# Normalisation of the later chunks moved into the steps of an expert layer, ranks from one comparison of all pairs

## The chip, the cores and the metric

The kernel runs on one core of a Trainium2 chip. The metric is the device time of one execution in microseconds (us), as the median of several runs. A core has five engines that work side by side and wait for each other through semaphores: TensorE (PE in the profile, with its weight loads as PEld), VectorE (DVE), ScalarE (ACT), GpSimd (POOL) and SyncE (SP, which here only issues DMAs). Each engine executes its own instructions in the order in which the program wrote them.

## The reference

x has 16 sequences of 128 tokens of width 128. Eight layers follow each other, each of the form x = x + tanh(gate) * f(layernorm(x)). The change concerns layer 0, a mixture of eight experts whose routing comes from the context, and the normalisation in front of layer 1, a feed-forward layer with quantised values.

```python
def _layernorm(x, axis=-1, eps=1e-05):
    m = jnp.mean(x, axis=axis, keepdims=True)
    v = jnp.var(x, axis=axis, keepdims=True)
    return (x - m) / jnp.sqrt(v + eps)
...
x = x + jnp.tanh(g_xattn[0]) * _L0_xattn_ref(_layernorm(x, axis=-1), ctx_1024, L0_xattn_Wg, L0_xattn_bg, L0_xattn_W1, L0_xattn_b1, L0_xattn_W2, L0_xattn_b2)
x = x + jnp.tanh(g_ffn[0]) * _L0_ffn_ref(_layernorm(x, axis=-1), L0_ffn_w1, L0_ffn_b1, L0_ffn_w2, L0_ffn_b2)
```

As the kernel computes layer 0: the logits of the eight experts are context times Wg plus a bias, for each token; the two experts with the highest logits are kept (the rank of an expert is the number of experts above it, a tie going to the lower number), the softmax over these two gives the weights `comb`; each expert is relu(n W1 + b1) W2 + b2, and the weighted sum over the experts, times tanh of the gate, is added to x.

## The kernel before

x is held transposed in `xT` (128 features on the partitions, 2048 tokens in the free dimension) and worked on in four chunks of 512 tokens. The normalised x is `nT`.

**Normalisation** (`pe_norm`, `act_norm`, `dve_norm`). For one chunk: PE multiplies by a centring matrix (L204), ACT squares the result into `nT` (L222), PE averages over the features (L209), ACT takes Ln and Exp to get one over the root (L226, L227), DVE multiplies (L235). Each float32 matmul of 512 columns is two instructions in the trace. In layer 0 DVE then splits the result into two float16 parts in `x16` (L241, L243; semaphores `s_hi`, `s_lo`). The four chunks are interleaved in the order of `ORDER`. In layers 0 and 1 all four chunks are normalised before the layer's own loop begins: `pe_norm` ends with a wait for all four.

**Layer 0** (`pe_moe`, `act_moe`, `dve_moe`) has 32 steps k, chunk c = k // 8 and expert e = k % 8. In step k PE makes 12 matmuls of 512 columns for the hidden values (`up`, L308), waits before each group of three that ACT has read that bank, and then the 48 matmuls of the second product of step k - 1 (`down`, L336). In the first step of a chunk PE waits for `s_lo`, the split part of that chunk. ACT reads each of the four banks twice, into float32 (L364) and float16 (L365). DVE subtracts the two to get the low part (`lo`, L378, `dve_moe_lo`), and adds the product of a step into `acc` with the expert's weight (L394 or L396). In DVE's loop the order of step k is: low part of the weights of expert k + 2 in chunk 0 (L284), low parts of step k + 1, wait for `down` of step k, accumulate step k. After the second step of the next chunk PE transposes `acc` and adds b2 (`pe_moe_out`, L349 and L350, eight pairs of 128 columns), and DVE updates `xT` (L405), which is `s_x`. In the fifth step of a chunk `comb` is transposed (L324), ACT copies it out one step later (L373).

The weights come in float32 through the four places of `stage`, and are split into float16 parts: the high part of expert 0 by DVE (L279) and of the others by ACT (L295), the low part by DVE (L284).

After step 0's `up` PE multiplies the context for the logits (L314). DVE adds the bias (L429), prepares the exponent (L432), and counts ranks with three small instructions for each expert (L437, L439, L441), 24 in all with a memset; then `lo` of step 1, the threshold, `comb` (L443 to L450), accumulation of step 0 and the low weights of expert 3.

**Layer 1** after its norm: per chunk 4 matmuls (L469), keys and values of layer 2 (L549, L551), the second product of the chunk before (L479). POOL gathers rows of a table in between, two in each step of layer 0, eight after it, and then spreads keys for layer 2 (L706).

SP issues all loads in the order of the program; the loads of experts 4 to 7 wait for a free place of `stage`.

## Time and profile before

| | |
|---|---|
| median of 3 runs | 948.12 us (942.97 to 950.73) |
| the profiled execution, device time | 939.63 us |
| its span from first to last instruction | 937.8 us |
| granted TensorE clock, mean | 0.931 of full |
| PE busy | 808.9 us, 86% of the span |
| DVE, ACT, POOL busy | 626.8, 570.3, 289.8 us |

Layer 0 with its norm fills the first 227 us of the span, layer 1 the time to about 265 us; the rest of the kernel, 673 us, is not edited. Busy times overlap: what sets the end is the chain of waits, followed from the last instruction back. A matmul's time depends on the granted clock, which has two levels, 1.2 and 2.4 GHz; 1.00 in a row is the upper one. Numbers of a profile are those of one execution.

### The profile page before, as it was taken

The numbers are of one execution on the slowest core, as the hardware profiler recorded it, in microseconds if no ns is written. First come the engines' busy times: TensorE is split into PE (matmuls) and PEld (weight loads), VectorE is DVE, ScalarE is ACT, GpSimd is POOL, SyncE is SP. The second block draws the span as 40 slices with busy tenths as digits, with TensorE's granted clock in tenths as the row PEclk, the third lists the DMA queues.
The fourth block names the chain that finished last, engine by engine and source line by source line (L and its number), as shares of the span: only waits on it lengthen the run. The fifth ranks groups of instructions, "written<-read, shape, count | busy, mean of one in ns | idle before, by whom it ended". The sixth has DMA issues, their size and how long they took to land.

```text
span 937.8 us, 14730 instructions
## 1 busy us (share of the span) xinstructions
PE 808.9 (86%) x5849; PEld 510.5 (54%) x5857; DVE 626.8 (67%) x994; ACT 570.3 (61%) x985; POOL 289.8 (31%) x253
## 2 busy tenths in 40 slices
PE   4899999999887888999939989968989868888775
PEld 1576767675433554555529656545668834444322
DVE  3896666663467778398784687854976246777567
ACT  5797878784664676545552433525588456666564
POOL 1043343432427777440030321034970012000003
PEclk9899999998997999999968997967999989999889
DMA  6121000002500001110000000060000000000001
GB/s 233 52 85 27 24 24 24 24 24 72 54 0 24 22 22 32 30 31 7 0 1 1 1 0 2 0 227 0 1 2 1 1 0 1 0 1 1 0 0 45
DMA packets 12852, 25.69 MB, mean 27 GB/s; under 512 B 3560, under 2 KB 4848, under 8 KB 12528
## 3 DMA queue, kind: packets, MB, share of 16 engines
q1 hardware_dynamic: 8688, 16.36, 6.0%
q0 software_dynamic: 4096, 8.40, 3.6%
q8 instruction: 46, 0.75, 0.4%
q14 instruction: 22, 0.18, 0.1%
HBM read 23.69 MB, written 1.05 MB: 26 GB/s over the span
## 4 chain that ended last, share of the span: by engine, by line
PE 58%; DVE 20%; ACT 12%; POOL 4%; issue 4%; DMA 1%; SPq 0%; DVEq 0%; POOLq 0%; ACTq 0%
PE ps L336 9%; PE ps L308 8%; PE ps L859 6%; PE ps L1025 3%; POOL big L706 2%; POOL pe L966 2%; PE ps L1377 2%; PE ps L204 2%; PE ps L578 2%; PE ps L1347 2%; DVE big L1112 2%; PE ps L469 2%; ACT nT L226 1%; ACT nT L227 1%; PE ps L1061 1%
## 5 line engine op out<-in xcount | busy, mean ns | idle before, releaser
L966 POOL DMA_INDIRECT pe<-in_rpe,idx x128 | 136.3, 1065 | 201.6 <-PE ps L336 114.1
L378 DVE TENSOR_TENSOR big<-l1f_w,big 128x512 f16<-128x512 f32 x128 | 87.4, 692 | 45.0 <-ACT big L365 42.8
L364 ACT ACTIVATE l1f_w<-ps,wcols 128x512 f32<-128x512 f32 x128 | 90.0, 703 | 32.8 <-PE ps L308 30.2
L308 PE MATMUL ps<-vx,big 128*128 128x512 f16 x384 | 94.7, 400 | 2.7 <-DVE nT L235 2.7
L336 PE MATMUL ps<-big 128*128 128x128 f16 x1536 | 92.6, 221 | 4.8 <-DVE big L378 4.8
L336 PEld LDWEIGHTS ps<-big 128*128 128x128 f16 x1536 | 89.9, 99 | 12.6 <-DVE big L378 5.5
L365 ACT ACTIVATE big<-ps,wcols 128x512 f16<-128x512 f32 x128 | 90.5, 707 | 0.0
L308 PEld LDWEIGHTS ps<-vx,big 128*128 128x128 f16 x384 | 38.1, 102 | 46.4 <-issue 8.7
L859 PE MATMUL ps<-nT,l1f_w 128*128 128x512 f32 x128 | 57.6, 592 | 0.0
L765 ACT ACTIVATE big<-ps 128x1024 f32<-128x1024 f32 x32 | 32.7, 1023 | 35.0 <-PE ps L575 35.0
L1642 POOL TENSOR_TENSOR big<-l1f_w,big 128x512 f16<-128x512 f32 x8 | 10.1, 1269 | 138.7 <-ACT big L1679 138.7
L1094 ACT ACTIVATE big<-ps,small 128x128 f32<-128x128 f32 x128 | 35.0, 379 | 26.3 <-PE ps L1052 26.2
L781 DVE TENSOR_REDUCE small<-ps 128x16 f32<-128x1024 f32 x32 | 38.8, 1218 | 8.8 <-PE ps L569 8.8
L204 PE MATMUL ps<-xT,consts 128*128 128x512 f32 x56 | 34.8, 729 | 11.3 <-DMA xT<-in_xT 10.3
L235 DVE TENSOR_TENSOR nT<-ps,nT 128x512 f32<-128x512 f32 x28 | 19.3, 690 | 37.2 <-ACT nT L227 37.2
L983 POOL TENSOR_TENSOR big<-nT,consts 128x512 f32<-128x512 f32 x16 | 17.4, 1098 | 84.8 <-PE ps L1042 44.5
L1025 PE MATMUL ps<-big,pe 128*128 128x128 f32 x256 | 32.3, 291 | 12.1 <-DVE big L1112 11.8
L578 PE MATMUL ps<-big 32*128 32x512 f16 x192 | 28.2, 399 | 15.8 <-POOL big L706 9.0
L886 ACT ACTIVATE big<-ps,wcols 128x1024 f32<-128x1024 f32 x16 | 17.9, 1116 | 39.0 <-PE ps L859 39.0
L1025 PEld LDWEIGHTS ps<-big,pe 128*128 128x128 f32 x256 | 31.8, 207 | 12.4 <-DVE big L1112 11.9
L1061 PEld LDWEIGHTS ps<-vx,big 128*128 128x128 f32 x256 | 34.2, 210 | 6.5 <-DVE big L1165 4.4
L209 PE MATMUL ps<-nT,consts 128*128 128x512 f32 x56 | 33.2, 677 | 3.7 <-ACT nT L222 3.6
(328 smaller groups left out, 1852.2 us busy)
## 6 DMA issues: line engine op xcount, KB each, us to landing
big<-in_l0x_w SPq DMA_DIRECT2D x16, 256.0 KB, 3.9
pe<-in_l2f_w SPq DMA_DIRECT2D x16, 256.0 KB, 6.4
pe<-in_rpe,idx POOLq DMA_INDIRECT x128, 2.6
cT<-in_cT SPq DMA_DIRECT2D x1, 1024.0 KB, 9.4
l1f_w<-in_l1f_w SPq DMA_DIRECT2D x1, 1024.0 KB, 5.1
vx<-in_ctok SPq DMA_DIRECT2D x1, 1024.0 KB, 16.7
out_xT<-xT SPq DMA_DIRECT2D x4, 256.0 KB, 2.3
xT<-in_xT SPq DMA_DIRECT2D x1, 768.0 KB, 7.5
```

The costliest lines, as they stand in the source:

```text
L204: te.matmul(bank(CEN[i] + c), centre_w, xT[:, cs(c)], start=True, stop=True).then_inc(s_cen, 1)
L308: mm = te.matmul(bank(f), w16[:, e, a, f * 128:(f + 1) * 128], x16[:, c, b, :], start=(n == 0), stop=(n == 2))
L336: mm = te.matmul(bank(4 + k % 2)[:, t * D:(t + 1) * D], h16[:, k % 2, a, f, t * S:(t + 1) * S], w16[:, k % E, b, F + f * D:F + (f + 1) * D ...
L364: act.activation(h32[:, f, :], bank(f), ACT.Relu, bias=b, scale=1 / W_UP)
L365: act.activation(h16[:, k % 2, 0, f, :], bank(f), ACT.Relu, bias=b, scale=1 / W_UP).then_inc(M0["act"], 1)
L378: dve.tensor_tensor(h16[:, k % 2, 1, f, :], h32[:, f, :], h16[:, k % 2, 0, f, :], SUB).then_inc(M0["lo"], 1)
L578: return te.matmul(bank(4 + t % 2), kT[quad(t), p, tok(b)], qblk1[quad(t), b % QS, r, :, :], start=(part == 0), stop=False)
L781: dve.tensor_reduce(mxp[:, b % 2, 2 * u:2 * u + 2, 0:8], ps[:, 1024 * u:1024 * (u + 1)].rearrange("p (t g k) -> p t g k", t=2, k=BLK), AX, ...
L859: mm = te.matmul(bank(at + r), l1f_w[:, w * D:(w + 1) * D], nT[:, cs(2 * (k // NC) + r)], start=True, stop=True)
L966: pool.indirect_dma_start(out=pe[:, v * D:(v + 1) * D], out_offset=None, in_=ins["rpe"], in_offset=bass.IndirectOffsetOnAxis(ap=idx[:, v:v ...
L1025: mm = te.matmul(bank(1 + f % 3)[:, j * 128:(j + 1) * 128], peT[:, f * VG + j, :], qblk[:, :, f * VG + j, :], start=True, stop=True)
L1061: mm = te.matmul(bank(6 + b % 2)[:, h * HW2:(h + 1) * HW2], cw[:, b % 2, h, :], vx4[:, b, h, :], start=True, stop=True)
```

## The change

In layer 0 only chunk 0 is normalised in front. Chunk c + 1 is centred in step e = 5 of chunk c (at its end on PE and on ACT) and averaged, turned into its factor and multiplied in step e = 6 (on DVE at the end of the loop's step, after the accumulation). The norm of layer 1 for chunk c - 1 stands in steps e = 2 and 3 of chunk c; that for the last chunk inside the first two rounds of layer 1's loop. Both use banks 6 and 7. `NORM_NO` numbers the eight norms in their new order.

The b2 product of `pe_moe_out` becomes one matmul of 512 columns instead of four of 128.

The ranks come from one comparison of all pairs (`above`, 1,024 elements a partition), seven small ones that replace "greater" by "greater or equal" where e is compared with a lower number, and one sum over 1,024 elements, which stands after the `lo` of step 1.

Loads: the constants needed in front come in a part of their own (192 KB of 440), with chunk 0 of x; expert 0's weights come next and have a semaphore of their own with the gates; then the context, experts 1 and 2, the gather's indices and the remaining constants, expert 3, and the rest of x. DVE makes the high part of expert 1's weights too. ACT's seven small copies of constants (L1775 to L1779) move from the start to behind layer 0.

```diff
@@ -184,12 +184,62 @@
         VAR = (2, 4, 6, 2, 0, 6, 0, 4)
         SPLIT = (0, 7)
 
+        NORM_NO = {(0, 0): 0, (0, 1): 1, (1, 0): 2, (0, 2): 3, (1, 1): 4, (0, 3): 5, (1, 2): 6, (1, 3): 7}
+
+        def late(k):
+            c, e = divmod(k, E)
+            if e in (5, 6) and c + 1 < NCH:
+                return ("cen", "var")[e - 5], 0, c + 1
+            if e in (2, 3) and c:
+                return ("cen", "var")[e - 2], 1, c - 1
+            return None, None, None
+
+        def pe_late_norm(te, k):
+            part, i, c = late(k)
+            if part == "cen":
+                n = NORM_NO[(i, c)]
+                if i:
+                    te.wait_ge(s_x, c + 1)
+                else:
+                    loaded(te, "x1")
+                    te.wait_ge(s_norm, n)
+                te.matmul(bank(6), centre_w, xT[:, cs(c)], start=True, stop=True).then_inc(s_cen, 1)
+            elif part == "var":
+                n = NORM_NO[(i, c)]
+                te.wait_ge(s_sq, n + 1)
+                if i == 0:
+                    te.wait_ge(M0["combT"], c)
+                te.matmul(bank(7), mean_w, nT[:, cs(c)], start=True, stop=True).then_inc(s_var, 1)
+
+        def act_late_norm(act, link, k):
+            part, i, c = late(k)
+            if part == "cen":
+                act.wait_ge(s_cen, NORM_NO[(i, c)] + 1)
+                act.activation(nT[:, cs(c)], bank(6), ACT.Square).then_inc(s_sq, 1)
+            elif part == "var":
+                act.wait_ge(s_var, NORM_NO[(i, c)] + 1)
+                link(act.activation(nT[:, cs(c)], bank(7), ACT.Ln, bias=eps5[:]))
+                act.activation(nT[:, cs(c)], nT[:, cs(c)], ACT.Exp, scale=-0.5).then_inc(s_rstd, 1)
+
+        def dve_late_norm(dve, k):
+            part, i, c = late(k)
+            if part == "var":
+                dve_scale(dve, i, c, bank(6))
+
+        def dve_scale(dve, i, c, centred):
+            n = NORM_NO[(i, c)]
+            dve.wait_ge(s_rstd, n + 1)
+            dve.tensor_tensor(nT[:, cs(c)], centred, nT[:, cs(c)], MUL).then_inc(s_norm, 1)
+            if i == 0:
+                dve.wait_ge(s_norm, n + 1)
+                dve.tensor_copy(x16[:, c, 0, :], nT[:, cs(c)]).then_inc(s_hi, 1)
+                dve.wait_ge(s_hi, c + 1)
+                dve.tensor_tensor(x16[:, c, 1, :], nT[:, cs(c)], x16[:, c, 0, :], SUB).then_inc(s_lo, 1)
+
         def x_done(layer, c):
             return NCH * layer + c + 1 if layer < 2 else 2 * NCH + BC * (c + 1) if layer == 2 else NCH * layer + B - NCH + c + 1
 
         def pe_norm(te, i, more=None):
-            if i == 0:
-                loaded(te, "const")
             if i == 4:
                 te.wait_ge(F3["best"], NC * NCH // 2)
                 te.wait_ge(F3["cand"], NC * NCH // 2)
...
@@ -274,10 +320,11 @@
             return ap.unsqueeze(2).to_broadcast([128, B, E])
 
 
-        def dve_first_parts(dve, link):
-            loaded(dve, "experts0", 4)
-            dve.tensor_scalar(w16[:, 0, 0, :], stage[:, 0, :], W_UP, None, MUL).then_inc(M0["w_hi"], 1)
-            dve_w_lo(dve, 0)
+        def dve_first_parts(dve, e):
+            if e:
+                loaded(dve, "experts0", 2)
+            dve.tensor_scalar(w16[:, e, 0, :], stage[:, e, :], W_UP, None, MUL).then_inc(M0["w_hi"], 1)
+            dve_w_lo(dve, e)
 
         def dve_w_lo(dve, e):
             dve.wait_ge(M0["w_hi"], e + 1)
...
@@ -317,9 +364,14 @@
                     pe_down(te, k - 1)
                 if e == 1 and c:
                     pe_moe_out(te, c - 1)
+                pe_late_norm(te, k)
                 if e == E // 2:
                     te.wait_ge(M0["comb"], 1)
                     te.wait_ge(X4["gkv"], 1)
+                    if c:
+                        te.wait_ge(s_rstd, NORM_NO[(1, c - 1)] + 1)
+                    else:
+                        loaded(te, "const")
                     for t in range(BC):
                         mm = te.transpose(ps[0:E, 3584 + t * S:3584 + (t + 1) * S], comb[:, c * BC + t, :], ident)
                     mm.then_inc(M0["combT_ps"], 1)
...
@@ -343,16 +395,21 @@
             te.wait_ge(M0["combT"], c + 1)
             if c:
                 te.wait_ge(s_x, c)
+                te.wait_ge(s_norm, NORM_NO[(1, c - 1)] + 1)
             loaded(te, "cols")
+            te.matmul(bank(6), l0x_b2[:], combT[:, cs(c)], start=True, stop=False)
             for t in range(BC):
-                dst = bank(6)[:, t * S:(t + 1) * S]
-                te.matmul(dst, l0x_b2[:], combT[:, tok(c * BC + t)], start=True, stop=False)
-                mm = te.matmul(dst, acc[:, t, :], ident, start=False, stop=True)
+                mm = te.matmul(bank(6)[:, t * S:(t + 1) * S], acc[:, t, :], ident, start=False, stop=(t == BC - 1))
             mm.then_inc(M0["out_ps"], 1)
 
-        def act_moe(act):
-            act.wait_ge(M0["w_hi"], 1)
-            act_w_hi(act, 1)
+        def act_moe(act, link):
+            act.wait_ge(s_set, 4)
+            act.wait_ge(s_cen, 1)
+            act.activation(nT[:, cs(0)], bank(4), ACT.Square).then_inc(s_sq, 1)
+            act.wait_ge(s_var, 1)
+            link(act.activation(nT[:, cs(0)], bank(2), ACT.Ln, bias=eps5[:]))
+            act.activation(nT[:, cs(0)], nT[:, cs(0)], ACT.Exp, scale=-0.5).then_inc(s_rstd, 1)
+            act.wait_ge(M0["w_hi"], 2)
             for k in range(NCH * E):
                 for f in range(FT):
                     act.wait_ge(M0["up"], FT * k + f + 1)
...
@@ -371,6 +428,7 @@
                 if k % E == E // 2 + 1:
                     act.wait_ge(M0["combT_ps"], k // E + 1)
                     act.activation(combT[:, cs(k // E)], ps[0:E, 3584:4096], ACT.Copy).then_inc(M0["combT"], 1)
+                act_late_norm(act, link, k)
 
         def dve_moe_lo(dve, k):
             for f in range(FT):
...
@@ -398,6 +456,7 @@
                 dve.wait_ge(M0["acc"], k + 1)
                 if e == 0 and c:
                     dve_moe_out(dve, c - 1)
+                dve_late_norm(dve, k)
             dve_moe_out(dve, NCH - 1)
 
         def dve_moe_out(dve, c):
...
@@ -406,21 +465,30 @@
 
 
         def pe_layer0(te):
-            pe_norm(te, 0)
+            loaded(te, "x0")
+            te.matmul(bank(4), centre_w, xT[:, cs(0)], start=True, stop=True).then_inc(s_cen, 1)
+            te.wait_ge(s_sq, 1)
+            te.matmul(bank(2), mean_w, nT[:, cs(0)], start=True, stop=True).then_inc(s_var, 1)
+            te.wait_ge(s_norm, 1)
             pe_moe(te)
 
         def act_layer0(act, link):
-            act_norm(act, link, 0)
-            act_moe(act)
+            act_moe(act, link)
+            loaded(act, "const")
+            act.activation(identb[:], ident, ACT.Copy).then_inc(s_g, 1)
+            act.activation(maskb[:], maskneg, ACT.Copy).then_inc(s_g, 1)
+            for j in range(4):
+                act.activation(keysb[:, j * S:(j + 1) * S], to_keys, ACT.Copy, scale=minus4[:, j:j + 1])
+            act.activation(hm16b[:], hm16, ACT.Copy).then_inc(s_g, 1)
 
         def dve_layer0(dve, link):
             loaded(dve, "cols")
-            loaded(dve, "gate")
+            loaded(dve, "gate_expert0")
 
             dve.tensor_tensor(ctx_w[:, E:], gate_w[:, 2 * NH2:4 * NH2], gate_w[:, 4 * NH2:6 * NH2], ADD).then_inc(X4["ctx_w"], 1)
-            dve_first_parts(dve, link)
-            dve_norm(dve, 0)
-            dve_w_lo(dve, 1)
+            dve_first_parts(dve, 0)
+            dve_scale(dve, 0, 0, bank(4))
+            dve_first_parts(dve, 1)
             dve_moe_lo(dve, 0)
             dve_w_lo(dve, 2)
             dve.wait_ge(M0["logit"], 1)
...
@@ -431,15 +499,13 @@
             link(dve.tensor_reduce(red, lg, AX, MAX))
             dve.tensor_tensor(ex, lg, per_b(red), SUB).then_inc(M0["exp_in"], 1)
 
-            link(dve.memset(sm(256), 0.0))
-            for e in range(E):
-                one = lg[:, :, e:e + 1]
-                link(dve.tensor_tensor(cmp, one.to_broadcast([128, B, E]), lg, ALU.is_gt))
-                if e < E - 1:
-                    link(dve.tensor_tensor(cmp[:, :, e + 1:], one.to_broadcast([128, B, E - 1 - e]),
-                                           lg[:, :, e + 1:], ALU.is_ge))
-                link(dve.tensor_tensor(rank, rank, cmp, ADD))
+            pairs = [128, B, E, E]
+            link(dve.tensor_tensor(above, lg.unsqueeze(2).to_broadcast(pairs), lg.unsqueeze(3).to_broadcast(pairs), ALU.is_gt))
+            for e in range(1, E):
+                ins_ = dve.tensor_tensor(above[:, :, e, 0:e], lg[:, :, 0:e], lg[:, :, e:e + 1].to_broadcast([128, B, e]), ALU.is_ge)
+            link(ins_)
             dve_moe_lo(dve, 1)
+            link(dve.tensor_reduce(rank, above, AX, ADD))
             link(dve.tensor_scalar(sm(256), sm(256), 2.0, None, ALU.is_lt))
             dve.wait_ge(M0["exp"], 1)
             link(dve.tensor_tensor(ex, ex, rank, MUL))
...
@@ -459,15 +525,21 @@
         o16 = work[:, 2048:2048 + CW].bitcast(f16).rearrange("p (r n) -> p r n", r=2)
 
         def pe_layer1(te):
-            pe_norm(te, 1)
             loaded(te, "l0f")
             for c in range(NCH + 1):
                 if c < NCH:
+                    te.wait_ge(s_norm, NORM_NO[(1, c)] + 1)
                     for f in range(FT):
                         if c:
                             te.wait_ge(F1["act"], FT * (c - 1) + f + 1)
                         te.matmul(bank(f), l0f_w1[:, f * 128:(f + 1) * 128], nT[:, cs(c)],
                                   start=True, stop=True).then_inc(F1["up"], 1)
+                    if c == 1:
+                        te.wait_ge(s_sq, 2 * NCH)
+                        te.matmul(bank(4), mean_w, nT[:, cs(NCH - 1)], start=True, stop=True).then_inc(s_var, 1)
+                    if c == 0:
+                        te.wait_ge(s_x, NCH)
+                        te.matmul(bank(5), centre_w, xT[:, cs(NCH - 1)], start=True, stop=True).then_inc(s_cen, 1)
                     pe_keys(te, c)
                 if c:
                     k = c - 1
...
@@ -475,13 +547,15 @@
                     te.wait_ge(F1["act"], FT * (k + 1))
                     if k >= 2:
                         te.wait_ge(F1["o16"], k - 1)
+                    else:
+                        te.wait_ge(s_norm, 2 * NCH)
                     for f in range(FT):
                         mm = te.matmul(bank(4 + k % 2), w2q[:, f, :], hq[:, k % 2, f, :],
                                        start=(f == 0), stop=(f == FT - 1))
                     mm.then_inc(F1["down"], 1)
 
         def act_layer1(act, link):
-            act_norm(act, link, 1)
+            last = nT[:, cs(NCH - 1)]
             loaded(act, "l0f")
 
             act.activation(w2q, l0f_w2.rearrange("p (t d) -> p t d", t=FT), ACT.Copy,
...
@@ -496,6 +570,13 @@
                             act.wait_ge(F1["down"], c - 1)
                         act.activation(hq[:, c % 2, f, :], bank(f), ACT.Relu, bias=col("l0f_b1", f),
                                        saturate=False).then_inc(F1["act"], 1)
+                    if c == 1:
+                        act.wait_ge(s_var, 2 * NCH)
+                        link(act.activation(last, bank(4), ACT.Ln, bias=eps5[:]))
+                        act.activation(last, last, ACT.Exp, scale=-0.5).then_inc(s_rstd, 1)
+                    if c == 0:
+                        act.wait_ge(s_cen, 2 * NCH)
+                        act.activation(last, bank(5), ACT.Square).then_inc(s_sq, 1)
                     act.wait_ge(A2["proj_ps"], 2 * c + 1)
                     act.activation(kT[:, 0, cs(c)], bank(6), ACT.Copy).then_inc(A2["hi"], 1)
                 if c:
...
@@ -506,8 +587,9 @@
                     act.activation(o16[:, k % 2, :], bank(4 + k % 2), ACT.Identity, bias=bq[:]).then_inc(F1["o16"], 1)
 
         def dve_layer1(dve, link):
-            dve_norm(dve, 1)
             for c in range(NCH + 1):
+                if c == 1:
+                    dve_scale(dve, 1, NCH - 1, bank(5))
                 if c < NCH:
                     dve_keys(dve, c)
                 if c:
...
@@ -1702,23 +1784,26 @@
         def _(sp):
             def load(k, dst, name, at=0):
                 sp.dma_start(dst, ins[name][:, at:at + dst.shape[-1]]).then_inc(s_load[k], 16)
-            sp.dma_start(idx[:], ins["idxT"]).then_inc(s_idx, 16)
-            load("const", consts[:], "consts")
+            load("cols", rows[:], "rows")
+            load("x0", consts[:, 256:640], "consts", 256)
             load("x0", xT[:, 0:CW], "xT")
             load("cols", wcols[:], "wcols")
-            load("cols", rows[:], "rows")
             load("cols", l0x_b2[:], "l0x_b2")
-            load("gate", gate_w[:], "gate_w")
+            load("gate_expert0", gate_w[:], "gate_w")
             for e in range(E):
                 if e == 1:
-                    load("x1", xT[:, CW:], "xT", CW)
-                if e == 2:
                     load("ctx", ctx_w[:, 0:E], "l0x_wg")
                     load("ctx", cT[:], "cT")
+                if e == 3:
+                    sp.dma_start(idx[:], ins["idxT"]).then_inc(s_idx, 16)
+                    load("const", consts[:, 0:256], "consts")
+                    load("const", consts[:, 640:], "consts", 640)
+                if e == 4:
+                    load("x1", xT[:, CW:], "xT", CW)
                 if e >= 4:
                     sp.wait_ge(M0["w16"], e - 3)
-                load("experts%d" % (e // 2), stage[:, e % 4, 0:F], "l0x_w1", e * F)
-                load("experts%d" % (e // 2), stage[:, e % 4, F:2 * F], "l0x_w2", e * F)
+                load("experts%d" % (e // 2) if e else "gate_expert0", stage[:, e % 4, 0:F], "l0x_w1", e * F)
+                load("experts%d" % (e // 2) if e else "gate_expert0", stage[:, e % 4, F:2 * F], "l0x_w2", e * F)
             load("l0f", l0f_w1, "l0f_w1")
             load("l0f", l0f_w2, "l0f_w2")
             load("l1x", l1x_w[:], "l1x_w")
...
```

## Rows read from the trace of the kernel before

**Rows 1.** Chain of waits, in order of time: start us, us, what.

```profile
4.82 7.52 DMA xT<-in_xT
...
48.07 2.59 PE ps L308 x12
50.66 2.68 PE ps L336 x48
...
85.39 0.41 PE ps L349 x2
85.81 0.42 PE ps L350 x2
...
88.73 4.26 PE ps L308 x12
...
117.19 2.59 PE ps L308 x12
...
226.84 3.41 PE ps L204 x4
...
238.94 5.29 PE ps L469 x8
```

**Rows 2.** Timeline of the first 50 us: start, duration, instruction, idle before and its releaser.

```profile
6.04 2.05 PE L204 MATMUL ps<-xT,consts 128*128 128x512 f32 x2 [6.04 <-DMA xT<-in_xT]
...
6.52 1.28 ACT L1774 ACT_TABLE_LOAD   x1
...
13.72 0.69 DVE L279 TENSOR_SCALAR big<-big 128x1024 f16<-128x1024 f32 x1 [6.39 <-DMA big<-in_l0x_w]
14.26 1.91 PE L209 MATMUL ps<-nT,consts 128*128 128x512 f32 x2
...
16.21 0.69 ACT L226 ACTIVATE nT<-ps,eps 128x512 f32<-128x512 f32 x1 [1.11 <-PE ps L209]
...
17.59 0.69 DVE L235 TENSOR_TENSOR nT<-ps,nT 128x512 f32<-128x512 f32 x1 [1.92 <-ACT nT L227]
...
18.77 0.69 DVE L243 TENSOR_TENSOR vx<-nT,vx 128x512 f16<-128x512 f32 x1
...
24.06 4.27 PE L308 MATMUL ps<-vx,big 128*128 128x512 f16 x12 [2.70 <-DVE nT L235]
...
33.50 0.29 DVE L432 TENSOR_TENSOR small<-small 128x128 f32<-128x128 f32 x1
...
34.29 0.27 DVE L439 TENSOR_TENSOR small<-small 128x112 f32<-128x112 f32 x1
...
38.02 0.73 ACT L365 ACTIVATE big<-ps,wcols 128x512 f16<-128x512 f32 x1
...
41.03 2.50 DVE L378 TENSOR_TENSOR big<-l1f_w,big 128x512 f16<-128x512 f32 x4
...
46.38 1.22 DVE L284 SCALAR_TENSOR_TENSOR big<-big 128x1024 f16<-128x1024 f32 x1
```

**Rows 3.** Timelines of DVE and of ACT in one steady step of chunk 1.

```profile
122.64 0.69 DVE L378 TENSOR_TENSOR big<-l1f_w,big 128x512 f16<-128x512 f32 x1 [0.46 <-ACT big L365]
123.25 1.12 DVE L396 SCALAR_TENSOR_TENSOR big<-ps,small,big 128x128 f32<-128x128 f32 x4
...
117.88 0.69 ACT L364 ACTIVATE l1f_w<-ps,wcols 128x512 f32<-128x512 f32 x1 [0.54 <-PE ps L308]
...
123.15 0.69 ACT L364 ACTIVATE l1f_w<-ps,wcols 128x512 f32<-128x512 f32 x1 [0.54 <-PE ps L308]
```

**Rows 4.** Timeline of 225 to 278 us, POOL's and PE's first work for layer 2.

```profile
253.25 5.62 POOL L706 TENSOR_TENSOR big<-big,consts 128x1024 f16<-128x1024 f16 x3
...
277.38 0.84 PE L569 MATMUL ps<-big,nT 32*128 32x512 f16 x12
```

**Rows 5.** Page, costliest groups: count, busy us, mean ns, idle before.

```profile
L781 DVE TENSOR_REDUCE small<-ps 128x16 f32<-128x1024 f32 x32 | 38.8, 1218 | 8.8 <-PE ps L569 8.8
```

**Rows 6.** Busy by stretch: us, PE, PEld, DVE, ACT, POOL busy (x), clock, DMA share, GB/s.

```profile
0.00:20.00 20.00, 9.66 (x14) 3.54 (x14) 4.18 (x7) 9.10 (x18) 2.60 (x10) 1.00 0.81 274
...
225.00:232.00 7.00, 7.00 (x13) 3.45 (x14) 0.75 (x1) 1.20 (x3) 2.21 (x3) 0.51 0.44 151
```

21 lines of the change are left out of this document (6 added, 15 removed).

## The prediction, made before the changed kernel was run

> **What bounds the kernel now.** I read the page first, then the chain of waits, then the timelines of the stretches that the diff touches. The chain goes through PE in all of layer 0 after its first steps: 12 matmuls of `up` take 2.59 us and 48 of `down` 2.68, with nothing between [rows 1], so a step is 5.27 us. ACT and DVE have a little room: in the step whose `up` starts at 117.19, ACT begins 0.69 later, DVE's last `lo` starts at 122.64 and its accumulation at 123.25, 0.79 after the next step's start [rows 1, 3]. Work added to PE in a step costs its full time, work added to ACT or DVE nothing until it makes PE wait. Three stretches aren't like that. Until 24.06 the chain waits for x (landing at 12.34) and then alternates between engines through four norms. From there to 48.07 it goes through DVE's logits, ranks and `lo` [rows 1, 2]. From 226.84 to 238.94 it goes through the norm of layer 1, 12.1 us [rows 1].
>
> **The front: saves 12.5 us.** Centring of chunk 0 started at 6.04 [rows 2]; with 468 KB ahead in place of 776, at the mean 274 GB/s of the first 20 us [rows 6], its data are there 1.1 us earlier; issue order gives less, so I take 5.5. It takes 2.05 us, until 7.55. The activation table was there at 7.80 [rows 2]; what released it is issued one place earlier, about half a microsecond. So ACT squares at 7.6 (0.6 us); averaging takes 1.91, until 10.1; Ln to the start of DVE's product took 17.59 - 16.21 = 1.38, until 11.5; product, copy and subtraction 19.46 - 17.59 = 1.87 [rows 2]. PE's `up` of step 0 starts at 13.5 in place of 24.06. Expert 0's parts need DVE for 0.7 + 1.22 us ahead of 11.5. All that is loaded up to there is 1.1 MB, about 4 us at that rate behind a start near 2 us, so DVE starts on them at 6.5 to 8.5 and is done in time.
>
> From `up` to the end of L432 it took 33.79 - 24.06 = 9.73 us [rows 2]. PE may run the whole first `up` at 1.2 GHz, at most 0.85 us more than its 4.27; I take 0.4, so 23.6. The ranks took from there to 41.03, 7.24 us [rows 2]. The comparison of all pairs is nearest to DVE's 1,024-element reduction, 1.22 us [rows 5], the seven small ones are at most 0.27 each [rows 2], in sum 3.1: 26.7. Now ACT decides: its last read of step 1 ended 4.96 us after L432 (38.75 - 33.79), so at 28.6, and `lo` 0.7 later, at 29.3, in place of 43.53 [rows 2]. Then come the sum over the pairs, 1.22 [rows 5], and as before 47.60 - 43.53 = 4.07 us until expert 3's low weights are there [rows 2]: 34.6. So `up` of step 3 starts at 34.65 in place of 48.07, 13.4 us earlier. PE will be idle for 2.6 us just ahead of it. After 3.9 us idle, `down` took 4.48 us in place of 2.68 (it began at 43.59). I charge half of that 1.8. Bounds: 10.5 (data of chunk 0 no earlier, clock lost) to 14.5.
>
> **Norms inside the steps: cost 10.3 us.** L204's four instructions took 3.41 us at 1.2 GHz, where the granted clock was 0.51 [rows 1, 6], so 0.43 each at the full clock, and each of a norm's two matmuls, two instructions, 0.86. Six norms (three of layer 0, three of layer 1) are 6 * 1.72 = 10.3 on an engine without gaps. ACT's 0.6 for the square, or 1.3 for Ln and Exp, fits: its eight reads take 4.7 of a step of now 6.1.
>
> **The wait at each chunk's start: costs 13.8 us.** This is the term that the rest turns on. In step 8 PE needs `s_lo` of chunk 1. DVE makes it at the end of its loop's step 6, behind the accumulation of step 6, which needs `down` of step 6, which PE issues in step 7 only. DVE also does the `lo` of step 7 first, and that needs ACT's reads of step 7, which stand behind Ln and Exp of the late norm. Averaging ends about 0.2 us after step 7's `up` starts; Ln and Exp then hold ACT until 1.45 after it, where it began at 0.69 before: 0.76 late. So the accumulation starts 6.06 + 0.76 = 6.82 after step 7's `up` (6.06 is 123.25 - 117.19 [rows 1, 3]), takes 1.14, and product, copy and subtraction 1.87 more plus 0.05: 9.88. PE is through with step 7 at 5.27. It waits 4.6 us, three times: 13.8. Behind PE's wait stand `up` of step 8 and all else; nothing else on PE can fill it. Without ACT's lateness it is 3.85, and without the `lo` in front 3.1: 9.3 in sum is the lower bound. At the fourth chunk's end there is no such wait.
>
> **The clock at these places: 0.2 us.** Before, the `up` that followed each `pe_moe_out` took 4.26 us in place of 2.59 [rows 1], at 1.2 GHz after 3.34 us of 128-column float32 pairs; three times, 5.0 us. With fewer of these I expect that to go. After the new waits of 4.6 us the same will come: the nearest rows are 1.7 (24.06, after 2.7 us idle) and 1.8 (43.59). So 5.2 comes for 5.0 that goes. The bounds are -5 (no slow stretch after the waits) and +10 (both kinds, and the new ones long, as from 225 to 232 where the granted clock was 0.51 for 7 us [rows 6]). The Trainium skill (TensorE: Matmul & The Clock Gate, "What's actually happening") puts the ramp penalty below 1% of a typical span. [...]
>
> **`pe_moe_out`: saves 4.0 us.** Eight pairs take 3.34; now 0.86 + 4 * 0.42 = 2.54 [rows 1], so 0.8 three times. The last one took 4.1 because it ran partly at 1.2 GHz; 1.5 there.
>
> **Layer 1: saves 9.0 us.** 12.1 of norm go. The last chunk's norm adds 1.72 and a wait: averaging to product takes 3.16 us, of which its own 0.86 and keys and values of 1.75 cover 2.61, so 0.55. The 1.2 GHz stretch that began at 225 [rows 6] now covers L469 in place of the norm; the first eight took 5.29 anyway [rows 1], at most 6.9 if it lasts as long: 0.8 more. So 12.1 - 2.3 - 0.8. What comes next isn't late: POOL's keys are ready at 258.9 after gathers that wait for the same `s_x`; PE asked for them at 277.38 [rows 4], now some 10 us earlier against it, 8 us of room.
>
> **Costed at nothing.** ACT's seven copies fall where ACT is idle for 10 us after layer 0; the rest of x is needed in step 5, 25 us after it lands; the context lands before 12 us, used at 18; indices come later but POOL's second gathers wait for step 0's `down` anyway. High weights of expert 1 on DVE sit ahead of `lo` of step 0, which ACT paces. Their cover gone, each costs a microsecond once.
>
> **Sum.** -12.5 + 10.3 + 13.8 + 0.2 - 4.0 - 9.0 = -1.2 us. Against the profiled execution's 939.63 that is 938.4; the median of the runs shown is 8.5 higher, so 948.1 - 1.2 = 946.9, rounded to 947.
>
> **Rivals.** (1) PE doesn't wait at the chunk starts: the split part of the next chunk is there in time. Then 13.8 and the 5.2 of clock go, 928. For it speaks only that DVE is idle a third of the time; against it the order of DVE's loop. It would take the multiplication one step earlier. (2) The clock ends on the other side: each of the three waits brings a slow stretch of some 7 us, not 3.4, and the one after `pe_moe_out` stays; +10, 957. For it the stretch of 225 to 232, which also followed idle time; against it the two single ones at 24 and 44. It decides (slower by over 1%) once PE loses 10.7 us more to the clock than my sum has. (3) Expert 0's weights land as late as before, at 13.72, since DMAs of many loads share the engines: DVE then starts `up` at 13.7 + 1.9 + 1.9 = 17.5, 4 us later, 951. Against it they have half the bytes in front of them.
>
> **How the numbers follow.** My forecast 0.62, (1) 0.14, (2) 0.14, (3) 0.10. A measurement here tells 1% from no change. My own case spans 940 to 954: front +/-2, wait -4.5, clock -5 to +5. (1) lies outside at 928 and is most of what I leave out; a tail of (2) above 957 is the rest. So 937 to 957 for 8 in 10. Faster by over 1% (below 938.6) is (1) and a little of my own case, 0.20; slower (above 957.6) is half of (2) and scatter, 0.12; same 0.68.
>
> **What would show it.** Front: first L308 at 13 to 14.5, the fourth `up` at 34 to 36. Steps: six pairs of 0.86. Chunk starts: PE idle before L308 of 4 to 5 us, released by DVE's subtraction, with `up` near 4.3 behind it. Layer 1: no norm in front. I am wrong if PE doesn't stand still at the starts of chunks 1 to 3, or if the clock takes another 10 us.

## The result, and the profile after

The changed kernel took 951.37 us (median of 20 runs, 947.98 to 954.35), the kernel before 944.61 us beside it (20 runs, 941.96 to 954.75). The ratio of the means is 1.0055, 95% interval 1.0033 to 1.0078: half a per cent slower, 5.2 us (6.8 between the medians, since the runs of the kernel before lie in a long tail above theirs), where 1.2 us less was forecast. Executions over 1.5% longer than the fastest of their kernel on a chip are left out of the ratios below; the one profile of the kernel before on the second chip is of such an execution (941.98 us). The profiled execution took 954.32 us, with a span of 952.5 us and a mean granted clock of 0.93; PE was busy for 810.0 us, DVE for 623.7, ACT for 569.7, POOL for 287.2. So the engines have the same work, and the time between lies elsewhere.

Two lines of the page, part 5 (count, busy us, mean ns, idle before and what ended it). L355 is `up` (L308 before), L847 reads the scores of layer 2 (L765 before):

```profile
L355 PE MATMUL ps<-vx,big 128*128 128x512 f16 x384 | 94.8, 400 | 19.3 <-DVE vx L237 16.9
...
L847 ACT ACTIVATE big<-ps 128x1024 f32<-128x1024 f32 x32 | 32.8, 1024 | 44.9 <-PE ps L657 44.6
```

PE stands still for 16.9 us ahead of `up` until DVE's subtraction L237 is done: 3.4 ahead of the first `up`, and three waits of 4.5 at the starts of chunks 1 to 3.

The timeline of the first 42 us, the rows that answer to [rows 2]:

```profile
4.85 2.08 PE L469 MATMUL ps<-xT,consts 128*128 128x512 f32 x2 [4.85 <-DMA xT<-in_xT]
...
13.20 4.34 PE L355 MATMUL ps<-vx,big 128*128 128x512 f16 x12 [3.44 <-DVE vx L237]
...
22.83 1.22 DVE L503 TENSOR_TENSOR small<-small 128x1024 f32<-128x1024 f32 x1
24.08 1.05 DVE L505 TENSOR_TENSOR small<-small 128x16 f32<-128x16 f32 x7
...
28.52 1.21 DVE L508 TENSOR_REDUCE small<-small 128x128 f32<-128x1024 f32 x1
...
33.99 2.76 PE L355 MATMUL ps<-vx,big 128*128 128x512 f16 x12 [2.43 <-DVE big L331]
```

The first `up` starts at 13.20 instead of 24.06, that of step 3 at 33.99 instead of 48.07. The comparison of all pairs is one instruction of 1.22 us, the seven small ones take 1.05 together, the sum 1.21.

The chain of waits around the start of chunk 1 and the first `pe_moe_out` (start us, us, what), for [rows 1]:

```profile
50.41 0.91 PE ps L206 x2
...
56.59 0.91 PE ps L212 x2
57.51 1.31 PE ps L355 x6
...
64.16 1.13 DVE big L454 x4
65.29 0.02 issue
65.32 0.70 DVE nT L232
66.02 0.02 issue
66.04 0.44 DVE vx L235
66.48 0.02 issue
66.50 0.70 DVE vx L237
67.20 0.05 issue
67.25 4.45 PE ps L355 x12
...
79.65 1.05 PE ps L400 x2
80.70 1.09 PE ps L402 x8
81.79 2.59 PE ps L355 x12
...
230.21 1.12 PE ps L400 x2
231.33 1.83 PE ps L402 x8
233.16 4.36 PE ps L535 x8
```

The chain runs through the accumulation L454, the late product L232, copy and subtraction, and only then into `up` of step 8, which takes 4.45 us at the lower clock. `pe_moe_out` takes 2.14 us, and `up` behind it 2.59. Layer 1's first matmul is at 233.16, where it was at 238.94 [rows 1].

And the timeline at the end of layer 1, where the surprise is. L598 is the x update (L516 before), L788 the key products on POOL (L706 before), L251 the centring for layer 2:

```profile
260.55 7.13 DVE L598 SCALAR_TENSOR_TENSOR xT<-big,gt,xT 128x512 f32<-128x512 f16 x2
...
261.50 5.62 POOL L788 TENSOR_TENSOR big<-big,consts 128x1024 f16<-128x1024 f16 x3
...
267.74 1.12 PE L251 MATMUL ps<-xT,consts 128*128 128x512 f32 x2 [2.48 <-DVE xT L598]
```

Two x updates take 7.13 us. By the view of that source line, the first takes 0.75 and the second 6.27: it ends 0.57 us after the last of POOL's three key products, which the row of L788 gives together, and the norm of layer 2 waits for it.

### The profile page after: what moved, and what is told of

It reads as the page before. It is cut to its first block, busy times and chain, and to the rows that moved or that the text cites. A ratio compares the mean times of both kernels' runs of the same rounds, so it can differ in the third digit from the quotient of the medians.

```text
span 952.5 us, 14681 instructions
## 1 busy us (share of the span) xinstructions
PE 810.0 (85%) x5833; PEld 505.3 (53%) x5833; DVE 623.7 (65%) x980; ACT 569.7 (60%) x984; POOL 287.2 (30%) x253
## 3 DMA queue, kind: packets, MB, share of 16 engines
HBM read 23.69 MB, written 1.05 MB: 26 GB/s over the span
## 4 chain that ended last, share of the span: by engine, by line
PE 61%; DVE 20%; ACT 13%; issue 4%; POOL 1%; DMA 1%; POOLq 0%; SPq 0%; DVEq 0%; ACTq 0%
PE ps L355 8%; PE ps L388 7%; PE ps L941 6%; PE ps L1107 3%; PE ps L660 3%; PE ps L1459 2%; DVE big L1194 2%; PE ps L677 2%; PE ps L1429 2%; PE ps L673 2%; PE ps L535 2%; PE ps L1143 1%; PE ps L657 1%; PE ps L687 1%; ACT big L847 1%
## 5 line engine op out<-in xcount | busy, mean ns | idle before, releaser
L1048 POOL DMA_INDIRECT pe<-in_rpe,idx x128 | 132.7, 1036 | 215.5 <-PE ps L388 134.1
L355 PE MATMUL ps<-vx,big 128*128 128x512 f16 x384 | 94.8, 400 | 19.3 <-DVE vx L237 16.9
L355 PEld LDWEIGHTS ps<-vx,big 128*128 128x128 f16 x384 | 38.6, 102 | 71.3 <-issue 18.4
L847 ACT ACTIVATE big<-ps 128x1024 f32<-128x1024 f32 x32 | 32.8, 1024 | 44.9 <-PE ps L657 44.6
L1107 PE MATMUL ps<-big,pe 128*128 128x128 f32 x256 | 31.0, 284 | 10.1 <-DVE big L1194 9.9
L788 POOL TENSOR_TENSOR big<-big,consts 128x1024 f16<-128x1024 f16 x16 | 30.4, 1904 | 27.4 <-PE ps L651 27.3
L1558 DVE TENSOR_TENSOR big<-small,big 128x528 f16<-128x528 f32 x32 | 26.6, 846 | 14.6 <-ACT big L1487 14.5
L941 PEld LDWEIGHTS ps<-nT,l1f_w 128*128 128x128 f32 x128 | 23.2, 190 | 23.9 <-issue 23.9
## 6 DMA issues: line engine op xcount, KB each, us to landing
vx<-in_ctok SPq DMA_DIRECT2D x1, 1024.0 KB, 16.9
```

What stands on the lines that cost most here:

```text
L355: mm = te.matmul(bank(f), w16[:, e, a, f * 128:(f + 1) * 128], x16[:, c, b, :], start=(n == 0), stop=(n == 2))
L847: act.activation(pr[:, b % 2, 2 * u:2 * u + 2, :, :].rearrange("p t j q -> p (t j q)"), ps[:, 2048:3072], ACT.Exp).then_inc(A2["exp"], 1)
L941: mm = te.matmul(bank(at + r), l1f_w[:, w * D:(w + 1) * D], nT[:, cs(2 * (k // NC) + r)], start=True, stop=True)
L1048: pool.indirect_dma_start(out=pe[:, v * D:(v + 1) * D], out_offset=None, in_=ins["rpe"], in_offset=bass.IndirectOffsetOnAxis(ap=idx[:, v:v ...
L1107: mm = te.matmul(bank(1 + f % 3)[:, j * 128:(j + 1) * 128], peT[:, f * VG + j, :], qblk[:, :, f * VG + j, :], start=True, stop=True)
```

## The experiments

Fifteen more runs were made, on four chips: e1 to e4 on the first, f1 to f4 on the second, g1 to g4 on the third, h1 to h3 on the fourth. On each chip the kernel before ran beside them, and ratios are to these runs. The changed kernel itself didn't run on the second chip, so what f2 and f4 are worth against it is a comparison of ratios between chips. Each expectation explains its theories; the ideas behind them are the forecast wait of PE for DVE at the chunk starts, the key products on POOL that hold the x updates, the clock behind the transposes, and a rhythm of layer 2 that belongs to the chip. Marks used below are starts on PE in the profiles: first `up`, first matmul of layer 1, first scores of layer 2, first matmul of layer 3.

### The changed kernel again, and each cause taken away

**The changed kernel, unedited.**

> The changed kernel once more, unedited, for a second profile on another chip. Layer 2 took 140.6 us in the first profile of it (from its norm's first matmul that waits for the last x, to the first matmul of layer 3) and 127.4 in the profile of before. Theory P (the change itself puts layer 2 into a slower rhythm): about 140 again, and the time about 1.01 of before. Theory Q (layer 2 has two rhythms whatever the kernel, and the profile fell in the slower one by chance): layer 2 may well take 127 here, with the profiled execution near 941; the timed ratio stays at 1.005.

Measured: 951.33 us, ratio 1.0057 (1.0028 to 1.0087). The result stands on another chip. Layer 2 is at the slower rhythm again, so both theories are still open here.

**The key products held back** until the last x update is done:

```diff
+            pool.wait_ge(s_x, 2 * NCH)
             for b in range(KS - 1):
                 pool_keys(pool, b)
```

> GpSimd's first two key products for layer 2 are held back until layer 1's four updates of x are done. In the profile of after the last two updates (one row, 7.13 us for two instead of 1.6) run at the same time as three key products of 5.6 us, and layer 2's norm waits for them until 267.74. Theory L (a VectorE operation with both inputs in SBUF stands still while GpSimd computes): the update takes 0.75 us each, layer 2's norm goes on at about 262.3, and the kernel is 5 us faster than after, ratio to before 1.000. Rival M (the update is late for another reason, its input or a queue): the long row stays and the time doesn't move, or the keys come too late for layer 2's first scores and the time is lost again there.

Measured: 949.57 us, ratio 1.0029 (1.0004 to 1.0053). The two x updates took 1.61 us together, so it was the products that held them. The scores started at 272.96, in the unedited kernel at 275.30 (0.7 of the 2.3 us was there at the start of layer 1 already). The gain is 2.6 us between the means of the runs, half of what theory L expected.

**The late product made before DVE's next `lo` and accumulation**, so that `s_lo` no longer waits for `down` of the same step:

```diff
                 if k and k + 2 < E:
                     dve_w_lo(dve, k + 2)
+                dve_late_norm(dve, k)
                 if 0 < k < NCH * E - 1:
                     dve_moe_lo(dve, k + 1)
...
-                dve_late_norm(dve, k)
```

> In VectorE's loop the late norm's product and split stand in front of the low parts of the next step instead of behind the accumulation. Theory W (TensorE stands still 4.6 us at the start of chunks 1 to 3 because of this order, and loses 1.8 to the clock each time afterwards): the three waits are gone and the kernel is 14 to 19 us faster than after. Rival V (the clock loss stays or comes back behind the transposes of the accumulator): 9 to 14 us. If the end of layer 1 still meets GpSimd's key products, the 5.5 us there stay.

Measured: 932.34 us, ratio 0.9871 (0.9825 to 0.9917). The chain of waits at the start of chunk 1, and at the end of layer 1:

```profile
54.49 2.68 PE ps L388 x48
57.17 0.91 PE ps L212 x2
58.09 2.59 PE ps L355 x12
60.68 2.68 PE ps L388 x48
63.36 2.59 PE ps L355 x12
...
240.51 1.74 PE ps L553 x8
...
242.99 6.23 DVE xT L598
249.27 1.12 PE ps L251 x2
```

The chunk starts with `up` straight behind `down`, at full clock. Layer 1 starts at 214.23 instead of 233.74, 19.5 us earlier. Three waits of 4.5 and three times 4.45 - 2.59 = 1.86 of clock are 19.1 (behind the first wait the unedited kernel took 5.00 on this chip, 0.5 more): the wait was what the prediction says it is. At 242.99 the x update meets the key products in full.

**Both edits.**

> Both edits. Theories L and W add up: 19 to 24 us faster than after, ratio to before about 0.982 to 0.985. Rival: GpSimd's gathers, which need the time of layer 0's steps and of layer 1, become what layer 2 waits for, and 5 us or more of it is not seen.

Measured: 927.51 us, ratio 0.9809 (0.9773 to 0.9845). From the start of layer 1 to the scores it took 39.1 us, in the kernel with the early product alone 43.1: where the products hit an x update in full they cost 4.0 us there.

### The parts alone, on a second chip

**The kernel before against itself.**

> The kernel before, unedited, for a second profile. Layer 2's loop has 16 turns; in the first profile of before a turn took 6.35 us and in five profiles with the change 7.17 to 7.27. Theory P (something in the change puts layer 2 into the slower rhythm): 6.35 here again. Theory Q (chance): some turns of 7.2 here too.

Measured: 931.02 us, ratio 0.9995 (0.9947 to 1.0044). On this chip the kernel before takes 932.48 us, 12 to 14 less than on the others.

**The change with the old eight pairs in `pe_moe_out`.**

```diff
-            te.matmul(bank(6), l0x_b2[:], combT[:, cs(c)], start=True, stop=False)
             for t in range(BC):
-                mm = te.matmul(bank(6)[:, t * S:(t + 1) * S], acc[:, t, :], ident, start=False, ...)
+                dst = bank(6)[:, t * S:(t + 1) * S]
+                te.matmul(dst, l0x_b2[:], combT[:, tok(c * BC + t)], start=True, stop=False)
+                mm = te.matmul(dst, acc[:, t, :], ident, start=False, stop=True)
```

> The changed kernel with the old form of the accumulator's transposes: eight pairs of 128-column float32 matmuls a chunk instead of one pair of 512 columns and four of 128. By the forecast's term it costs 0.8 us four times, 3.2, and if the slow clock stretch behind the transposes of chunks 0 to 2 comes back (1.7 each) 5 more: 8. Rival: no slow stretch, since the one behind PE's new waits has taken its place; 3. It also gives TensorE nearly the old number of instructions ahead of layer 2: if the length of its program is what slows layer 2's turns, they are 6.35 us again and the kernel is over 10 us faster.

Measured: 942.01 us, ratio 1.0135 (1.0097 to 1.0173). Layer 1 starts at 237.79, in three profiles of the changed kernel at 233.7, 4.1 later; three times 3.34 - 2.14 = 1.2, and 3.44 instead of 2.95 for the last group, are 4.1. `up` behind the eight pairs still took 2.59 (at 82.95), so the slow clock there isn't theirs alone: as the rival says, no slow stretch came back. The ratio is 0.8% above the changed kernel's on the other chips, 7 us; the profile shows 4.1 of it, and where the rest would lie isn't known.

**The kernel before with the new `pe_moe_out` and nothing else.**

> The kernel before with the new form of these transposes alone. The forecast's term: 0.8 us four times and the slow clock stretches behind three of them, 8 us faster than before in all (ratio 0.991). Rival: the stretches stay, 3 us (0.997). If this edit alone slows layer 2's turns to 7.2 us, it is 13 us slower instead.

Measured: 920.85 us, ratio 0.9892 (0.984 to 0.9944). Chain of waits:

```profile
84.58 1.05 PE ps L347 x2
85.63 1.09 PE ps L349 x8
86.72 2.59 PE ps L308 x12
...
216.45 2.44 PE ps L204 x4
218.88 0.97 PE ps L209 x2
...
226.78 5.40 PE ps L468 x8
```

Layer 1 starts at 226.78 instead of 238.52 in the profile of the kernel before on this chip. The first `up` was 0.3 earlier in this execution, the four groups of transposes are 4.7 us shorter, the `up` behind three of them 1.7 each, 5.0, and the norm at 216 is 1.7 shorter (3.41 + 1.72 before, 2.44 + 0.97 here): 11.7 us. The profile that this is held against has all its slow stretches, and not every execution has them (h1 below). The timed runs decide the worth: 11.6 us between the medians, 10.1 by the ratio (5 to 15). So this small part gains alone about twice what the whole change loses.

**The change with the old rank loop.**

```diff
-            pairs = [128, B, E, E]
-            link(dve.tensor_tensor(above, ..., ALU.is_gt))
-            for e in range(1, E):
-                ins_ = dve.tensor_tensor(above[:, :, e, 0:e], ..., ALU.is_ge)
-            link(ins_)
+            (the three small instructions for each expert, as before)
...
-            link(dve.tensor_reduce(rank, above, AX, ADD))
```

> The changed kernel with the old rank comparison of 24 small instructions. The forecast: the fourth up of layer 0 starts at 34 with the new ranks and 3.1 + 1.2 us of them on VectorE; the old ones take 7.24 before the low parts of step 1 in place of 2.3, so it starts some 4 to 5 us later, at 38 to 39, and the kernel is 4 to 7 us slower (7 with a slow clock stretch after the longer idle time). Rival: hidden, within 1 us, since ScalarE paces the low parts. Layer 2's turns tell by the way whether VectorE's program matters for them.

Measured: 937.97 us, ratio 1.0107 (1.0054 to 1.0159). `up` of step 3 starts at 37.16 instead of 33.99 (34.4 and 34.5 in other profiles of the changed kernel): the new ranks are worth about 3 us at that place. In the whole it would be 5 us by the ratios, but the interval reaches down to the changed kernel's own 1.0055.

### Which part of the difference is the chip's

In all four profiles of the second chip a turn of layer 2's loop takes 6.35 us, in the profile of the changed kernel and all of the first chip 7.2, and in the one of the kernel before 6.35. On the third chip both kernels were profiled side by side.

> The kernel before, unedited, profiled on the same chip as the changed kernel in this call. So far every profile of the first experiments' chip had layer 2 turns of 7.2 us and every one of the second's 6.35, with different kernels on each. Theory C (the chip decides): this profile and the next have the same turn, whichever it is. Theory P (the change decides): 6.35 here, 7.2 in the next.

Measured: 948.8 us in the one run, span 946.8, scores at 275.14, layer 3 at 403.19, a turn 7.2 us.

> The changed kernel, unedited. Theory C: turns of layer 2 as in the profile of before on this chip, and the timed difference of 5 us comes from elsewhere: from the updates of x that meet GpSimd's key products (5.5) and from the mean of the clock. Theory P: turns of 7.2 us, layer 2 about 13 us longer than before's.

Measured: 951.71 us, ratio 1.006 (1.003 to 1.0089); span 949.9, scores at 275.41, layer 3 at 406.87, a turn 7.2 us.

So the change doesn't make the rhythm: the kernel before has it here too. All profiles of one chip have the same, so it goes with the chip; each chip was used at one time only, so the hour isn't ruled out. ACT's reads of layer 2 in the page of this run of the kernel before, beside 35.0 us of idle time in the page of its first profile:

```profile
L765 ACT ACTIVATE big<-ps 128x1024 f32<-128x1024 f32 x32 | 32.8, 1024 | 45.2 <-PE ps L575 45.1
```

The first two profiles differ by 14.7 us in span, and this is most of it: from the first scores to layer 3 they take 114.8 and 130.7 us. On one chip it is 3.1 between the spans. Where these 3.1 arise is seen from the first matmuls of layer 3, in the timelines of g1 and of g2:

```profile
403.19 3.60 PE L859 MATMUL ps<-nT,l1f_w 128*128 128x512 f32 x8
```

```profile
406.87 3.60 PE L941 MATMUL ps<-nT,l1f_w 128*128 128x512 f32 x8
```

At the scores the changed kernel is only 0.3 us behind; from there to layer 3 it takes 131.5 us and the kernel before 128.1. In this profile of the changed kernel there is a stretch of low clock near the end of layer 2 (0.57 from 379 to 382 us), in that of the kernel before none.

> The changed kernel with GpSimd's key products behind the updates of x, on this chip. Theory L: 5 us faster than the changed kernel; rival, from the first measurement of it: 2 us.

Measured: 948.74 us, ratio 1.0041 (1.0007 to 1.0075). The timelines of the changed kernel and of this one, in this order:

```profile
259.44 5.62 POOL L788 TENSOR_TENSOR big<-big,consts 128x1024 f16<-128x1024 f16 x3
261.51 4.77 DVE L598 SCALAR_TENSOR_TENSOR xT<-big,gt,xT 128x512 f32<-128x512 f16 x2
```

```profile
261.93 1.62 DVE L598 SCALAR_TENSOR_TENSOR xT<-big,gt,xT 128x512 f32<-128x512 f16 x2
...
263.63 5.62 POOL L788 TENSOR_TENSOR big<-big,consts 128x1024 f16<-128x1024 f16 x3 [4.09 <-DVE xT L598]
```

In the changed kernel the products began 2 us before the updates here, so they held the first update for less: it took 4.11 us (view of the line) instead of 6.27. To take them away gains 1.0 us at the scores (274.39), 2.5 at layer 3 (404.41), and 3.2 between the means of the runs. Neither 5 nor 2, the two values expected.

> Both edits on this chip: 0.98 of before again, some 24 us faster than the changed kernel.

Measured: 927.87 us, ratio 0.9821 (0.977 to 0.9873), 24.4 us between the means, as expected.

### Does the kernel before pay for the products, and what is left

**The kernel before with its key products held back** by the same line.

> The kernel before, with POOL's layer-2 key products held until the last x update of layer 1 is done: nothing is left out. Theory K (the products cost the changed kernel time that they did not cost before, because there the x updates they hold have PE work behind them): in the kernel before they meet the first or second x update (3.1 to 6.6 us instead of 0.75), while PE still has an up of layer 1 to do, so to take them away gains nothing: ratio 0.998 to 1.002, start of layer 2's scores unchanged within 0.5 us, or later if the late keys become the last thing the scores wait for. Theory D (the products cost both kernels the same): about 2 to 3 us faster than before, 942 to 945 where before is 945 to 947, as in the changed kernel.

Measured: 945.81 us, ratio 0.9986 (0.9948 to 1.0023). From the start of layer 1 to the scores it took 38.5 us, as in the three profiles of the kernel before (38.4, 38.4 and 38.3). So up to the scores the products cost the kernel before nothing, as the first theory says; the interval of the timed ratio is too wide to rule out the 2 to 3 us of the second by itself. Its profile shows one thing more. The chain of waits at the start of chunk 3 and at the norm of layer 1:

```profile
182.78 0.41 PE ps L349 x2
183.19 0.42 PE ps L350 x2
183.61 2.59 PE ps L308 x12
...
224.13 1.72 PE ps L204 x4
225.85 0.97 PE ps L209 x2
...
233.74 5.40 PE ps L469 x8
```

Up to here this kernel does what the kernel before does, with the same instructions of PE, ACT and DVE. Yet `up` behind the third transposes takes 2.59 instead of 4.28, the norm 2.69 instead of 5.13, and layer 1 starts at 233.74 instead of 238.94. The granted clock isn't the same in each execution of the same work.

> The changed kernel once more, for comparison in one call. Theory P (what is left of its loss once the key products are gone is one stretch of low clock more near the end of layer 2, at 379 us, which comes with the hour at which its last turns fall): ratio 1.005 to 1.0075 where a turn of layer 2 takes 7.2 us, with the low stretch at 379 to 382 and its turn of 9.5 us there again; where a turn takes 6.35 us the stretch is missing, as in the two kernels with the change that ran at this rhythm, and the ratio is 1.002 to 1.004. Theory F (a fixed cost of the change): 1.0055 at either rhythm.

Measured: 952.15 us, ratio 1.0055 (1.0023 to 1.0088). Layer 1 at 233.67, scores at 275.20.

> The changed kernel with the key products held until the last x update, once more. Theory P: at 7.2 us a turn again 1.003 to 1.0045, with one low stretch near the end of layer 2; at 6.35 us a turn no such stretch and 0.997 to 1.001. Theory F: 1.0035 at either rhythm, so 2 us better than the changed kernel in the same call.

Measured: 947.67 us, ratio 1.0001 (0.9966 to 1.0037). Layer 1 at 233.77, scores at 274.19. The stretch of low clock near the end of layer 2 is in both (from 379.9 and 376.4 us), but also, from 375.0, in the kernel before with late products. So it can come without the change. Theory P expected 1.003 or more for this kernel, theory F 1.0035; 1.0001 speaks against both, but its interval reaches to 1.0037. The three ratios of this kernel, 1.0029, 1.0041 and 1.0001, each with some 0.003 to either side, agree with each other. Whether the change makes such a stretch more frequent stays open: at the rhythm of 7.2 us all four profiles of the changed kernel take 130.6 to 131.5 us from the scores to layer 3, the one of the kernel before 128.1, and that of the kernel before with held products (h1) 130.1.

## Why the prediction was wrong, point by point

**The step that failed** is the last sentence on layer 1: "What comes next isn't late: POOL's keys are ready at 258.9", with 8 us of room. It asked when the products are needed, and not whom they hold while they run. [rows 4] had the products, 5.62 us on POOL; the timeline of the kernel before has the x update of 6.64 us beside them, which I hadn't taken up:

```profile
252.79 6.64 DVE L516 SCALAR_TENSOR_TENSOR xT<-big,gt,xT 128x512 f32<-128x512 f16 x1
253.25 5.62 POOL L706 TENSOR_TENSOR big<-big,consts 128x1024 f16<-128x1024 f16 x3
```

There it was hidden: PE had the `up` of the last chunk to do, and the next update began at 261.08. The change starts layer 1 earlier against POOL's gathers, whose end sets the start of the products. So they now fall on the last updates, behind which PE has nothing but the norm of layer 2. Holding them back gives 2.6, 3.2 and 4.0 us between the means of the runs on three chips, 3.3 on average, and nothing up to the scores in the kernel before. The cost at the scores is 4.0 us where they hit one update in full (with the early product, with and without the products) and 1.0 where they hit it in part (the third and fourth chip). At layer 3 it is 2.0 to 2.5 in the three pairs of profiles: the part between the scores and layer 3 comes with the products too, but no row shows how.

That leaves 5.2 - 3.3 + 1.2 = 3.1 us of the miss. What is shown of it: the first `up` of the kernel before starts at 22.65 to 23.64 in three other profiles, not at 24.06, so the front saved 0.4 to 1.4 us less than against the profile I used. What is argued: this execution of the kernel before had every stretch of low clock that the sum takes as gone; another (h1) had two fewer and was at layer 1 5.2 us earlier, level with the changed kernel. How many executions are like it isn't known, since it lost the time again later. Of the timed runs of the kernel before outside the second chip 57 of 94 are below 947 us and the others reach up to 954.84; of 53 runs of the changed kernel none is below 947. What the record does show is that this goes with the mean granted clock of the run. Of 73 runs of the kernel before on the first, third and fourth chip, the 25 with a clock of 0.935 or more took 939.6 to 945.8 us and the 10 with 0.926 or less took 951.4 to 954.8; of the 53 runs of the changed kernel only three reached 0.935, and they took 949.8 to 950.2, while its seven at 0.926 or less took 952.2 to 955.2. So the changed kernel is slower where the clock is granted well, and nearly level where it isn't. Nothing was edited to test this, so it stays a correlation, and with it some 2 us of the miss stay open. On the third chip, the only one with profiles of both kernels, the loss lies behind the first scores, in layer 2, a part that the forecast took as unchanged because it isn't edited.

**The front** was right: 13.20 and 33.99 for 13.5 and 34.65. The ranks are about 3 us of it; the seven small comparisons took 0.15 us each, where the sum had 0.27.

**Norms in the steps** take 0.91 for each pair of instructions instead of 0.86, 10.9 us instead of 10.3.

**The wait at the chunk starts** was right in place, cause and size: 4.49 us of idle time each ((16.9 - 3.44) / 3) for 4.6, and taking it away gives back 19.0 us, the wait and the clock behind it. Rival 1, that PE doesn't wait, is refuted.

**The clock** went as forecast: 1.86 behind each wait for 1.7 (2.4 to 2.65 behind the first one in three other profiles), and nothing behind three of the `pe_moe_out`. That the last stretch also covers L402 and L535 was allowed for (0.8). Rival 2 (another 10 us) didn't come: the chain shows 4.45 behind each wait, at most 5.24 in the other profiles of the changed kernel. The loss below 1% of a span that the forecast names beside this term isn't what the trace shows: in the first 240 us of the kernel before, the stretches at 1.2 GHz cost (4.27 - 2.59) + (4.48 - 2.68) + (4.26 - 2.59) + 2 * (4.28 - 2.59) + (5.13 - 2.69) = 11.0 us against the same work at the upper clock, 1.2% of the span. Rival 3 (late weights) is refuted by 13.20.

**`pe_moe_out`** had its saving undersized: 2.14 us for 2.54, since a transpose takes 0.27 (1.09 for four) where I had 0.42 from its two instructions in a pair; 4.7 us in all for 4.0. And its worth with the clock is more than I gave the part: alone it makes the kernel 10 to 12 us faster. I had the 5.0 of it beside the 4.0, but not the 1.7 at the norm of layer 1, which the change then removes anyway.

**Layer 1** starts 1.5 us earlier than the sum has it (238.94 - 12.5 + 10.3 + 13.8 + 0.2 - 4.0 - 12.1 = 234.6), and PE is done with it at 260.67. From there on the x update takes 6.28 us. From the start of layer 1 to the scores the forecast added 3.1 us to the 38.4 of before (its 2.3 + 0.8); it took 44.3 in this profile, 41.5 to 41.7 in three others, and 40.4 to 40.6 with the products held back on the third and fourth chip. So the term without the products was a little high, and in three of four profiles the scores come within 1 us of the 276.2 that the sum gives. That hides the miss: the profile used as before has its scores at 277.38, the latest of four (the others: 276.94, 275.14, and 272.25 in h1).

The time lies within the range given, and within 1% of before, by far the likeliest case; but the sign was wrong. That the total came within 5 us is in part luck: the layer started 1.5 us early against the sum, and the held update took more than that back.

Read together with the Trainium skill: its page "SBUF — State Buffer", section "SBUF: two separate sides", says that VectorE and GpSimd share a pair of ports under an exclusive lock, which a VectorE operation with two inputs in SBUF needs too when GpSimd reads SBUF, and that the loser stands still for the whole instruction. The trace agrees that it stands still (0.75 us becomes 6.27), and goes further: the update didn't get in between POOL's three products of 1.9 us each, but ended 0.57 us after the third. In the rows it even began first, 0.08 us before the first product here and 0.46 us in the kernel before, and was held all the same. This rule would have told me to lay the two rows beside each other.

## What to carry to other kernels

When work is moved, don't only ask whether the next stage's input is ready in time; list what the other engines do in the new place of the critical instructions, and above all whether POOL works on SBUF while DVE makes what PE waits for. A product in front of a stage belongs ahead of work that depends on the running stage: moving it up by a few lines is worth 19 us here. And try a small part alone before it is bundled with large ones: the one matmul for four makes the kernel 1.1% faster by itself, the bundle is 0.5% slower, and the bundle with both repairs is 1.8 to 1.9% faster (927.51 us, 0.9809, and 927.87, 0.9821), the best ratio of this study. And take more than one profile of the kernel before: here three of them differ by 2.2 us at the scores, and a fourth that does the same up to there (h1) by 5, as much as the change is worth.

## What the runs showed of the hardware

- A DVE operation with two operands in SBUF took 0.75 us alone and up to 6.64 us while POOL multiplied; it ended 0.56 to 0.57 us after the last of three POOL instructions that followed each other without a gap, in each of the profiles looked at.
- The same program goes at one of two rhythms, which goes with the chip: a turn of layer 2 takes 6.35 us on one and 7.2 on three others, 12 to 14 us over the kernel. In the slower one ACT starts one of its two reads of a turn 0.8 us later behind the same matmuls (idle 1.66 to 1.71 us ahead of L765 or L847, instead of 0.84), and DVE's reduction behind them waits too. Why is open.
- Executions of the same instructions, on different chips, differ by 5 us at one place (233.74 and 238.94 at the start of layer 1), most of it by the granted clock, with 4.28 or 2.59 us for the same twelve matmuls behind the same eight transposes. On one chip the timed runs of one kernel reach from 939.6 to 952.8 us, the longer the lower their mean clock (0.941 and 0.925 at the ends). A forecast against one profile takes that execution's luck with it.
